# Output projection and inner layer of a dense stage in three fp32r products, with the third norm's turn, the roots and the moments in another order

## The reference, cut to what matters

```python
o = o.reshape(b, n, n, D) @ W_out                 # output projection, 256 x 256
h = layer_norm(x + o, ln_agg_g, ln_agg_b)         # first norm (H)
m = jax.nn.relu(h @ W1 + b1) @ W2 + b2            # inner layer 256 x 512, outer layer 512 x 256
t = layer_norm(m + h, ln2_g, ln2_b)               # second norm (T)
t + attention(_ln_t(t), ...)                      # third norm (X), computed here too and stored turned
```

## Time and profile before

| | us |
|---|---|
| median of 3 runs | 4137.0 |
| lowest and highest | 4132.11, 4137.24 |
| the profiled execution | 4140.06 |
| its span in the trace | 4138.3 |
| mean granted TensorE clock | 0.964 of full speed |
| dense stage in it | some 1219.7 to 1584.8 |

### The profile page before, as it was taken

The page is one execution under the profiler, slowest core; times in us unless marked ns, Lnnn a source line. Parts: engine busy times, 40 slices in busy tenths (PEclk is TensorE's granted clock), DMA queues, the critical chain, the costliest instruction groups (busy, mean ns, idle before and its releaser), DMA issues. The chain is left out here.

```text
span 4138.3 us, 80479 instructions
## 1 busy us (share of the span) xinstructions
PE 3626.7 (88%) x29887; PEld 2981.7 (72%) x29887; DVE 2923.9 (71%) x4176; ACT 2330.6 (56%) x5708; POOL 1374.5 (33%) x730
## 2 busy tenths in 40 slices
PE   8873888688869997999999979999999787788897
PEld 5541666466648886888888878888888644688886
DVE  2657999799966774577777755777777644577787
ACT  2422777577754554566656655566666401477776
POOL 0355999799964552100000011000000000122254
PEclk9986999899989998999999999999999899999999
DMA  4355111411122333000000021000000133554565
GB/s 124 93 152 148 43 42 42 110 44 41 42 56 87 107 103 106 21 16 16 16 16 26 11 71 41 16 16 16 16 16 11 40 132 132 164 137 135 146 201 174
DMA packets 210637, 303.42 MB, mean 73 GB/s; under 512 B 18624, under 2 KB 156736, under 8 KB 209728
## 3 DMA queue, kind: packets, MB, share of 16 engines
q1 hardware_dynamic: 201152, 291.51, 23.6%
q10 hardware_dynamic: 9216, 8.39, 0.6%
HBM read 199.18 MB, written 100.66 MB: 72 GB/s over the span
## 5 line engine op out<-in xcount | busy, mean ns | idle before, releaser
L631 POOL TENSOR_TENSOR mp_Z<-mp_lvs,mx_rv 128x1280 f32<-128x1280 f32 (+1 forms) x256 | 796.1, 3615 | 63.1 <-ACT mp_lvs L554 38.5
L611 DVE TENSOR_TENSOR mp_Z<-mp_psL,mx_rv 128x2816 f32<-128x2816 f32 (+1 forms) x256 | 783.9, 3139 | 46.6 <-DMA mx_rv<-rv 25.1
L561 ACT ACTIVATE mp_cut<-mp_psO,mx_mask 128x128 f32<-128x128 f32 x2048 | 551.7, 406 | 155.1 <-PE mp_psO L504 155.1
L504 PE MATMUL mp_psO<-mp_Z,mp_pair 128*16 128x256 f32 x8192 | 502.7, 387 | 107.3 <-POOL mp_Z L631 94.9
L1198 PE MATMUL sv_psO<-at_v_hi,sv_p_hi 128*128 128x258 f32 x2048 | 583.2, 285 | 13.3 <-DVE sv_p_lo L1286 10.1
L1198 PE MATMUL sv_psO<-at_v_lo,sv_p_hi 128*128 128x258 f32 x2048 | 578.1, 282 | 0.0
L1198 PE MATMUL sv_psO<-at_v_hi,sv_p_lo 128*128 128x258 f32 x2048 | 577.6, 282 | 0.0
L504 PEld LDWEIGHTS mp_psO<-mp_Z,mp_pair 128*16 128x16 f32 x8192 | 338.5, 124 | 247.6 <-DVE mp_Z L611 136.0
L1217 ACT COPY sv_S<-sv_psS 128x512 f32<-128x512 f32 x512 | 300.8, 588 | 379.8 <-PE sv_psS L1172 265.7
L1261 DVE TENSOR_TENSOR sv_run<-sv_run,sv_S 128x512 f32<-128x512 f32 x448 | 314.5, 702 | 249.7 <-ACT sv_S L1217 249.1
L1286 DVE TENSOR_TENSOR sv_p_lo<-sv_S,sv_p_hi 128x512 fp32r<-128x512 f32 x512 | 354.0, 691 | 107.3 <-ACT sv_p_hi L1226 105.4
(11 more groups left out here) (221 smaller groups left out, 7080.0 us busy)
## 6 DMA issues: line engine op xcount, KB each, us to landing
re_xg<-xg SPq DMA_DIRECT2D x192, 384.0 KB, 3.3
xg<-ga_xg SPq DMA_DIRECT2D x32, 768.0 KB, 3.7
mp_pair<-att SPq DMA_DIRECT2D x128, 128.0 KB, 2.6
fr_xr<-in_x SPq DMA_DIRECT2D x16, 512.0 KB, 4.4
fr_xl<-in_x SPq DMA_DIRECT2D x32, 256.0 KB, 4.2
rv<-fr_rvs SPq DMA_DIRECT2D x16, 512.0 KB, 3.0
att<-mx_rv SPq DMA_DIRECT2D x16, 512.0 KB, 7.0
att<-fr_E SPq DMA_DIRECT2D x16, 512.0 KB, 6.6
```

Source lines behind the costliest of these rows:

```text
L504: mm = pe.matmul(psO[32 * j:32 * j + 2 * H, c % 2, q, :], pair[:, s, :, :, c * YC + y], Z[:, c, y, :], start=True, stop=True, tile_positio ...
L561: ins = nc.scalar.activation(cut[:, s, c, :, h * DK:(h + 1) * DK], psO[:, c % 2, :, h * DK:(h + 1) * DK], ACT.Copy, scale=mask[:, h:h + 1])
L611: nc.vector.tensor_tensor(Z[:, c, 0:m], psL[:, s, 0:D].unsqueeze(1).broadcast_to([P, m, D]), rv[:, c * YC:c * YC + m, :], ALU.mult).then_i ...
L631: nc.gpsimd.tensor_tensor(Z[:, c, m:YC], lvs[:, s, :].unsqueeze(1).broadcast_to([P, YC - m, D]), rv[:, c * YC + m:(c + 1) * YC, :], ALU.mu ...
```

## The change

- The weights of output projection and inner layer, the turned o and the turned h are each cut into a high part (ScalarE writes it as fp32r) and a low part (VectorE subtracts the high part from the float32 value, also fp32r). Each product becomes three: high by high, high by low, low by high. That is 12 instead of 8 instructions on PE for the output projection and 24 instead of 16 for the inner layer. The outer layer stays in float32.
- The turned h is no longer shifted by b1n. Its part of the result, b1n @ W1, is made once ahead of the loop by 8 products of one column and added to b1 (`b1s`).
- PE's step becomes: turn h (i-1), output projection (i), turn o of the next tile (i+1), outer layer (i-2), turn x (i-5), inner layer (i-1).
- ScalarE: high part of h, the second norm's root, high part of the next tile's o, copy of the turned x, roots of first and third norm, relus, x norm.
- VectorE: the low part of h goes between the second norm's moments and its scaling, the low part of the next tile's o behind the residual.
- `xoff` is computed by two tensor_scalar instead of one scalar_tensor_tensor.
- SP issues the loads of tiles 0 and 1 ahead of the loop, and in step i those of tile i+2.

```diff
@@ sync @@
+                load(0)
+                load(1)
                 for i in range(LAST + 1):
-                    if i < NT:
-                        reach(sp, o_turned, i - 1)
-                        reach(sp, added1, i - 1)
...
+                    if i + 2 < NT:
+                        load(i + 2)
@@ tensor @@
+                def parts(k):
+
+                    return ((0, 0, k), (0, 1, k), (1, 0, k))
...
+                for f in range(MT):
+                    for k in range(KT):
+                        mm = pe.matmul(ps_m[:, f, 0:1], wa[:, k, f * P:(f + 1) * P], b1nc[:, k:k + 1], start=(k == 0), stop=(k == KT - 1))
+                mm.then_inc(b1_turned, 1)
...
+                turn_o(0)
                 for i in range(LAST + 1):
-                    if i < NT:
-                        pe.wait_ge(in_[i % 2], (i // 2 + 1) * 48)
-                        reach(pe, oT_kept, i)
-                        turn(ps_o, oin[:, i % 2], o_turned)
                     n = i - 1
                     if 0 <= n < NT:
                         pe.wait_ge(ln[H_LN]["normed"], n + 1)
                         reach(pe, hT_kept, n)
                         turn(ps_h, hn[:, n % 2], h_turned)
+                    if i < NT:
+                        pe.wait_ge(oT_kept, i + 1)
+                        reach(pe, added1, i)
+                        reach(pe, w_cut, 1)
+                        for u in range(U):
+                            terms = [t for k in range(KT) for t in parts(k)]
+                            for e, (a, c, k) in enumerate(terms):
+                                mm = pe.matmul(ps_1[:, u * D:(u + 1) * D], oTs[a][:, i % 2, k, u * P:(u + 1) * P], wos[c][:, k, :],
+                                               start=(e == 0), stop=(e == len(terms) - 1))
+                        mm.then_inc(made1, 1)
+                    if i + 1 < NT:
+                        turn_o(i + 1)
+                    n = i - 2
+                    if 0 <= n < NT:
+                        pe.wait_ge(mT_made, n * 2 + 2)
+                        reach(pe, added3, n)
+                        by_token(ps_3, mT[:, n % 2], wb, MT, made3)
                     n = i - 5
...
                         turn(ps_x, xl[:, n % 2], x_turned)
-                    if i < NT:
-                        pe.wait_ge(oT_kept, i + 1)
-                        reach(pe, added1, i)
-                        by_token(ps_1, oT[:, i % 2], wo, KT, made1)
                     n = i - 1
                     if 0 <= n < NT:
                         pe.wait_ge(hT_kept, n + 1)
...
+                            terms = [t for k in range(KT) for t in parts(k)]
+                            for e, (a, c, k) in enumerate(terms):
+                                mm = pe.matmul(ps_m[:, f, :], was[c][:, k, f * P:(f + 1) * P], hTs[a][:, n % 2, k, :],
+                                               start=(e == 0), stop=(e == len(terms) - 1))
@@ scalar @@
+                nc.scalar.copy(wo_hi[:, :, :], wo[:, :, :]).then_inc(w_hi_cut, 1)
+                nc.scalar.copy(wa_hi[:, :, :], wa[:, :, :]).then_inc(w_hi_cut, 1)
...
                         for k in range(KT):
-                            ins = nc.scalar.activation(hT[:, n % 2, k, :], ps_h[:, k * W:(k + 1) * W], ACT.Identity,
-                                                       bias=b1nc[:, k:k + 1], scale=g1c[:, k:k + 1])
-                        ins.then_inc(hT_kept, 1)
+                            ins = nc.scalar.activation(hT_hi[:, n % 2, k, :], ps_h[:, k * W:(k + 1) * W], ACT.Copy, scale=g1c[:, k:k + 1])
+                        ins.then_inc(hT_hi_kept, 1)
                     n = i - 3
                     if 0 <= n < NT:
                         root(T_LN, n)
+                    if i + 1 < NT:
+                        keep_oT_hi(i + 1)
@@ vector @@
+                def keep_oT_lo(n):
+                    dve.wait_ge(oT_hi_kept, n + 1)
+                    nc.vector.tensor_tensor(oT_lo[:, n % 2], ps_o[:, :].rearrange("p (k t) -> p k t", k=KT), oT_hi[:, n % 2], ALU.subtract).then_inc(oT_kept, 1)
+
+                def keep_hT_lo(n):
+                    dve.wait_ge(hT_hi_kept, n + 1)
+                    for k in range(KT):
+                        ins = nc.vector.scalar_tensor_tensor(out=hT_lo[:, n % 2, k, :], in0=ps_h[:, k * W:(k + 1) * W], scalar=g1c[:, k:k + 1],
+                                                             in1=hT_hi[:, n % 2, k, :], op0=ALU.mult, op1=ALU.subtract)
+                    ins.then_inc(hT_kept, 1)
...
                         moments(T_LN, n, t0[:, n % 2])
+                    n = i - 1
+                    if 0 <= n < NT:
+                        keep_hT_lo(n)
+                    n = i - 3
+                    if 0 <= n < NT:
                         reach(dve, t_scaled, n - 1)
                         normalise(T_LN, n, tn[:, n % 2], t0[:, n % 2])
...
                         nc.vector.tensor_tensor(h0[:, i % 2], tiles(ps_1), xres[:, i % 2], ALU.add).then_inc(added1, 1)
+                        if i + 1 < NT:
+                            keep_oT_lo(i + 1)
                         dve.wait_ge(added1, i + 1)
                         moments(H_LN, i, h0[:, i % 2])
...
-                        nc.vector.scalar_tensor_tensor(out=xoff[:, n % 2], in0=mv[:, X_LN, n % 2, :, 0:1], scalar=-1.0, in1=rstd[:, X_LN, n % 2],
-                                                       op0=ALU.mult, op1=ALU.mult).then_inc(xoff_made, 1)
+                        for u in range(U):
+                            ins = nc.vector.tensor_scalar(xoff[:, n % 2, u], mv[:, X_LN, n % 2, u, 0:1], rstd[:, X_LN, n % 2, u, :], -1.0, ALU.mult, ALU.mult)
+                        ins.then_inc(xoff_made, 1)
```

More of the change, by code:

```diff
@@ L657, in dense_phase @@
         wb = ph.sb("wb", [P, MT, D])
+        wo_hi, wo_lo = (ph.sb(n, [P, KT, D], F32R) for n in ("wo_hi", "wo_lo"))
+        wa_hi, wa_lo = (ph.sb(n, [P, KT, F1], F32R) for n in ("wa_hi", "wa_lo"))
         g1r, b1nr, b2r, hbr, g2r, b2nr = (ph.sb(n, [P, D]) for n in ("g1r", "b1nr", "b2r", "hbr", "g2r", "b2nr"))
@@ L730, in _, with load @@
                 ox = o_d.rearrange("b n (y x) d -> (b n) x y d", x=2)
-                for i in range(LAST + 1):
-                    if i < NT:
-                        reach(sp, o_turned, i - 1)
-                        reach(sp, added1, i - 1)
-                        for c in range(2):
-                            sp.dma_start(oin[c * N:(c + 1) * N, i % 2], ox[i * U:(i + 1) * U, c].rearrange("u y d -> y u d")).then_inc(in_[i % 2], 16)
-                        sp.dma_start(xres[:, i % 2], tile_rows(x.rearrange("b x y d -> (b x y) d"), i)).then_inc(in_[i % 2], 16)
+                def load(i):
+                    reach(sp, o_turned, i - 1)
+                    reach(sp, added1, i - 1)
+                    for c in range(2):
+                        sp.dma_start(oin[c * N:(c + 1) * N, i % 2], ox[i * U:(i + 1) * U, c].rearrange("u y d -> y u d")).then_inc(in_[i % 2], 16)
+                    sp.dma_start(xres[:, i % 2], tile_rows(x.rearrange("b x y d -> (b x y) d"), i)).then_inc(in_[i % 2], 16)
+                load(0)
+                load(1)
+                for i in range(LAST + 1):
+                    if i + 2 < NT:
+                        load(i + 2)
                     n = i - 4
@@ L762, in by_token, with turn_o @@
                     mm.then_inc(done, 1)
+                oTs, wos, hTs, was = (oT_hi, oT_lo), (wo_hi, wo_lo), (hT_hi, hT_lo), (wa_hi, wa_lo)
                 pe.wait_ge(w_in, 16 * len(loads))
+                for f in range(MT):
+                    for k in range(KT):
+                        mm = pe.matmul(ps_m[:, f, 0:1], wa[:, k, f * P:(f + 1) * P], b1nc[:, k:k + 1], start=(k == 0), stop=(k == KT - 1))
+                mm.then_inc(b1_turned, 1)
+                def turn_o(i):
+                    pe.wait_ge(in_[i % 2], (i // 2 + 1) * 48)
+                    reach(pe, oT_kept, i)
+                    turn(ps_o, oin[:, i % 2], o_turned)
+                turn_o(0)
                 for i in range(LAST + 1):
-                    if i < NT:
-                        pe.wait_ge(in_[i % 2], (i // 2 + 1) * 48)
-                        reach(pe, oT_kept, i)
-                        turn(ps_o, oin[:, i % 2], o_turned)
                     n = i - 1
@@ L789, in _ @@
                                 reach(pe, mT_made, (n - 1) * 2 + f // 2 + 1)
-                            for k in range(KT):
-                                mm = pe.matmul(ps_m[:, f, :], wa[:, k, f * P:(f + 1) * P], hT[:, n % 2, k, :], start=(k == 0), stop=(k == KT - 1))
+                            terms = [t for k in range(KT) for t in parts(k)]
+                            for e, (a, c, k) in enumerate(terms):
+                                mm = pe.matmul(ps_m[:, f, :], was[c][:, k, f * P:(f + 1) * P], hTs[a][:, n % 2, k, :],
+                                               start=(e == 0), stop=(e == len(terms) - 1))
                             if f % 2 == 1:
```

(13 more changed lines are left out.)

23 lines of the change are left out of this document (16 added, 7 removed).

## The result

The changed kernel took 4112.19 us (median of 4 runs, 4110.49 to 4112.92) against 4137.12 for the kernel before (4 runs). The ratio is 0.9940, with a 95% interval from 0.9923 to 0.9957: 18 to 32 us less, or 0.6%. In a later comparison on another chip it was 4106.07 (5 runs) against 4139.48 (11 runs), ratio 0.9921 (0.9907 to 0.9936). The profiled execution took 4112.46, that is 27.6 less than the one before.

What follows compares the result with a forecast made beforehand. The prediction took TensorE's time as the dense stage's bound, before and after. Gains of 29.5 us in the steps, 0.5 in filling and 2.6 in draining, 32.6 in all, gave 4104 us, range 4096 to 4120.

Steps and rivals of the forecast that it cites:

- The price of the parts: TensorE, output projection and inner layer: 0.1137 us a part product, plus 0.06 at each of three meetings of transposes and product.
- VectorE's work: VectorE, per tile: low part of o 0.60 us, of h 0.80, two offset instructions 0.25; 7.6 in all, under 9.05.
- The loop of waits: TensorE, ScalarE and VectorE over two steps: 18.1 us, 9.04 a step, 8.95 with overlap, just under TensorE's 9.05.
- rival (a): ScalarE's and VectorE's loop decides the dense stage's period: 9.3 to 9.6 us, total 4115; chance 0.20.
- The new waits costed at nothing: ScalarE's x copy, SP's loads and the outer layer wait in the new order, covered by 0.7, 1.1 and 1.3 us.
- The steps between: Dense stage from the third step: three steps of 8.61 us and 26 of 9.05, 261.1 for 290.67, gain 29.5.
- The filling: Dense stage's start: first turn 1.3 us later, low part of o 0.7, cheaper products give back 2.5; third step 0.5 earlier.
- (b): Dense stage's tile loads come late: at 1 us more landing time, period 9.3 us, total 4111; chance 0.05.
- (c): Late x turn holds ScalarE's roots and eats the gain: period 9.8 us and more, total 4130 to 4137; chance 0.05.
- (d): TensorE's 36 part products a tile: weight loads not hidden, +88 to +170 us, 4225 to 4307; 0.05 with (e) and (f).
- (e): Recurrence repeats a run because rounding changes, 186 us each, total 4290; chance 0.05 together with (d) and (f).
- (f): VectorE's two subtractions queue behind GpSimd's products, 1.1 us each: period 10.15, total 4141; 0.05 with (d) and (e).

Runs made afterwards that it cites:

- order_f32: The changed kernel with both products left in float32 and no low parts, so the new order alone: 4141.29 us.
- x_turn_after_o: The changed kernel with the third norm's turn directly behind the turn of o, ahead of the outer layer: 4110.17 us.
- old_xoff: The changed kernel with the third norm's offset as one scalar_tensor_tensor again: 4108.68 us.
- high_only: The changed kernel without the two low products of each three on TensorE, so part of the result is missing: 4088.60 us.
- work_in_loop: The changed kernel with four more VectorE tensor_scalar of 128x256, results unused, directly behind the low part of h: 4130.50 us.
- x_turn_early: The changed kernel with the third norm's turn put back directly behind the turn of h: 4152.05 us.

## Why the prediction was right, and where it was not

The forecast was 4104 with a range of 4096 to 4120. The median of the first comparison, 4112.2, lies in the range, 8 above the forecast; the second comparison's gain of 33.4 is near the forecast's 32.6, but its third step came 1.9 later after the first load than the forecast had it (33.9 for 32.0), so that nearness is chance in part.

**The bound before and after.** Right. TensorE without a hole at the full clock in both, period forecast 9.05, measured 9.04.

**The price of the parts.** The sum was right and its terms were not. I took 0.1137 a part product and 0.06 for each change between turns and products. Measured: 0.119 a part product and no price for a change: order_f32 adds up without it, x_turn_after_o has one change less and the same period. Where a turn meets part products, the turn takes 0.35 instead of 0.44 and the first interval 0.20 instead of 0.12, which cancel. 36 x 0.005 = 0.18 is what 3 x 0.06 had been meant to cover. A right period for a wrong reason, and by luck to 0.01.

**VectorE's work.** Forecast 0.60 and 0.80 for the low parts and 0.25 for the offset; measured 0.60, 0.79, 0.25; in all 7.4 a step, where 7.6 was forecast. Of the 192 subtractions in the earlier trace rows only 62 run beside a GpSimd instruction, so they bore the reading on fewer cases than it said; the changed kernel bears it out, since the low part of o (1402.94, 0.60 to the next start) lies inside GpSimd's product of 1402.50 to 1403.78. That the long offset goes is true; that it matters was never part of the sum, and old_xoff shows that it does not.

**The loop of waits.** The mechanism was right (the high part of h behind relus and x norm, the low part behind it), its length was not: I put it at 8.95 to 9.04 and gave rival (a) 0.20. In the changed kernel the scaling of h ends at 1397.28 and TensorE takes it at 1397.93, so two steps of 18.08 have 0.6 to spare: 8.74 a step (an estimate from the one gap). The term that was mis-sized is ScalarE's 2.96 for relus, x norm and high part: 0.84 + 1.09 + 1.03 were added without their overlap, and the high part takes 0.83, not 1.03: second relus to the end of the high part, 1398.13 to 1400.67, is 2.54. VectorE's terms add up to 5.72, not the 5.82 of the sum, and measure 5.60 (1400.71 to 1406.31). And I overlooked the loop that closes in one step, 8.30, which high_only and work_in_loop show. Both lie under 9.04, so neither is late; but the next limit is only 0.3 away.

**The new waits costed at nothing.** Right in the steady part, by the margins given: no wait of TensorE there. The turn of x has the least freedom, as x_turn_early shows.

**The steps between.** From the third step to step 31 I forecast 261.1; it is 1254.52 to 1515.46, 260.9. Draining, from step 31 to the last copy's end: forecast 36.9 - 2.6 = 34.3, measured 1549.50 + 0.59 - 1515.46 = 34.6.

**The filling.** Here the prediction failed. I forecast the third step 0.5 earlier; it came 2.4 later in the profiled execution. Three of its terms were right: the first turn 1.7 late by the bias products and the loads (forecast 1.3), 0.65 for the low part of o before the first product (0.7), and the cheaper products of steps 0 and 1 give back 0.84 + 0.70 + 0.94 = 2.5, as forecast. The step of the working that fell is "the low part of o adds 0.7 before the first product": it adds again in each of the first two steps, where nothing hides it. In step 0 the residual starts at 1241.96 and the moments at 1243.97, 2.01 later instead of 0.73, since the low part of the next o, waiting for its high part, stands between them; from the end of the first output projection to the turn of h TensorE takes 4.70 instead of 3.44, 1.26 more. In step 1 the same delay makes TensorE wait again: the turn of h that opens the third step starts 0.70 after the last part product would have let it. And the turn of the third tile's o now lies in step 1, at the half clock, 0.71 that I put at nothing. From the stage's first load the forecast put the third step at 32.0, and the kernels that fill alike have 33.4 to 35.0, so 1.4 to 3.0 of the miss are filling, 3.0 in the profiled execution; with the 1.7 that unchanged stages took more there and 0.3 of draining, that is the 5 between the forecast 32.6 and the profiled 27.6. The further 2.7 to the median's 24.9 lie within its interval.

**Rivals.** (b) did not occur, but high_only shows it from a step of about 8.3 on. (c) did not occur. (d) is refuted: 0.119 between starts with loads of 0.19. (e): the recurrence kept its 192 steps. (f): the two subtractions took no longer than forecast; its 4141 was also too high, since 1.1 a step over 29 steps is 32, that is 4136.

## What to carry to other kernels

Cutting the busiest engine's work pays only if the operands' new stages are made a step ahead: here parts alone kept 0.2 of 0.97 and order alone 0.06. After a period is computed, look for loops of waits through in-order queues, in one step and in two, and add them with the overlaps of neighbours; their length says what the next cut is worth. Size the filling by its own chain: a stage that the steady part hides was paid here again in each of the first two steps.

## What the runs showed that I had not expected

With TensorE relieved to some 6.2 us of work in a step of 8.3 to 8.5, the clock falls at times, here behind waits of 1.53 and 0.58: the mean granted clock was 0.95 in 1400 to 1500 of high_only, and one product of 16 took 4.84 instead of 3.62. In the draining the same waits left the clock full in one kernel and halved it for most of a product in two others. And four equal tensor_scalar took 1.38 or 1.82 us by their place beside GpSimd's products.
